# Attention of a graph and transformer kernel: the column-tiled matmuls of two steps put into one run behind the second, with a fourth buffer of weights

## What is computed

```python
q, k, v = (to_heads(q), to_heads(k), to_heads(v))
...
scores = jnp.einsum('bhqd,bhkd->bhqk', q, k) / jnp.sqrt(jnp.float32(HD))
causal = jnp.tril(jnp.ones((s, s), dtype=bool))
scores = jnp.where(causal, scores, -jnp.inf)
attn = jax.nn.softmax(scores, axis=-1)
y = jnp.einsum('bhqk,bhkd->bhqd', attn, v)
```

## Time and profile before

| | us |
|---|---|
| runs shown: median (lowest, highest) | 2546.53 (2538.53, 2550.58) |
| the profiled execution, its own time | 2537.73 |
| its span, first to last instruction | 2535.6 |
| TensorE busy, share of the span | 2115.2, 83% |
| VectorE busy | 1512.0, 60% |
| ScalarE busy | 1079.2, 43% |
| GpSimd busy | 533.2, 21% |
| mean granted clock of TensorE | 0.911 of full |

### The profile page before, as it was taken

The page is one execution under the profiler, slowest core; times in us unless marked ns, Lnnn a source line. Parts: engine busy times, 40 slices in busy tenths (PEclk is TensorE's granted clock), DMA queues, the critical chain, the costliest instruction groups (busy, mean ns, idle before and its releaser), DMA issues. The chain is left out here.

```text
span 2535.6 us, 42650 instructions
## 1 busy us (share of the span) xinstructions
PE 2115.2 (83%) x18144; PEld 1240.5 (49%) x18144; DVE 1512.0 (60%) x2332; ACT 1079.2 (43%) x1062; POOL 533.2 (21%) x442
## 2 busy tenths in 40 slices
PE   6799999999976799499999999974840599999990
PEld 3444444444432443244444444431440588888880
DVE  7778888888848169666666666601443343443423
ACT  5678888888832311023444444550210222322210
POOL 0000000000010024324555555562304000000005
PEclk9899999999988899679999999996855699999995
DMA  6311111211133213450040310007102533333307
GB/s 250 133 41 70 52 54 70 70 44 62 53 138 141 83 75 125 122 111 18 18 101 18 84 35 18 10 12 163 58 0 104 182 129 109 112 108 113 112 25 269
DMA packets 85341, 221.56 MB, mean 87 GB/s; under 512 B 9760, under 2 KB 10912, under 8 KB 78336
## 3 DMA queue, kind: packets, MB, share of 16 engines
q1 hardware_dynamic: 74064, 176.76, 21.8%
q0 software_dynamic: 11088, 42.08, 4.6%
HBM read 154.98 MB, written 59.51 MB: 85 GB/s over the span
## 5 line engine op out<-in xcount | busy, mean ns | idle before, releaser
L449 ACT ACTIVATE m_step<-m_ub,gat_bias 128x2048 bf16<-128x2048 f32 x256 | 493.9, 1992 | 119.3 <-DVE m_mask L526 105.4
L1087 DVE TENSOR_REDUCE t_rm<-t_m 128x1 f32<-128x512 f32 (+3 forms) x640 | 375.7, 609 | 203.4 <-PE t_m L1136 127.7
L1047 ACT ACTIVATE t_E<-t_s 128x1024 f32<-128x1024 f32 (+3 forms) x320 | 277.7, 894 | 368.6 <-PE t_s L1156 185.9
L526 DVE TENSOR_TENSOR m_mask<-m_step,gat_adjT 128x2048 bf16<-128x2048 bf16 x256 | 306.9, 1223 | 83.6 <-ACT m_step L449 73.4
L1026 POOL TENSOR_TENSOR t_total<-t_E 128x1024 f32<-128x1024 f32 (+2 forms) x160 | 307.8, 1936 | 167.2 <-PE t_d L1180 167.2
L1136 PE MATMUL t_m<-t_K,t_Q 96*128 96x512 f32 (+3 forms) x640 | 275.4, 452 | 55.7 <-DMA t_K<-scratch_parts 33.6
L1136 PEld LDWEIGHTS t_m<-t_K,t_Q 96*128 96x128 f32 x640 | 125.6, 200 | 208.2 <-DVE t_rm L1087 126.9
L566 PE MATMUL m_bd<-m_mask,m_S 128*32 128x512 bf16 x3072 | 211.3, 379 | 8.1 <-DVE m_mask L526 7.8
L566 PE MATMUL m_bd<-gat_adjT,m_S 128*32 128x512 bf16 x3072 | 211.3, 379 | 4.8 <-PE m_dn L566 4.8
L566 PE MATMUL m_bd<-m_mask,m_neg 128*32 128x512 bf16 x3072 | 211.1, 379 | 0.0
L1153 PE MATMUL t_s<-t_Q,t_K 97*128 97x512 f32 (+3 forms) x640 | 208.8, 402 | 0.5 <-ACT t_E L1047 0.5
(11 more groups left out here) (277 smaller groups left out, 3245.0 us busy)
## 6 DMA issues: line engine op xcount, KB each, us to landing
a_adj<-in_adj SPq DMA_DIRECT2D x16, 1024.0 KB, 5.0
m_ub<-scratch_uac SPq DMA_DIRECT2D x16, 1024.0 KB, 4.7
e_w1r<-in_L_ffn_w SPq DMA_DIRECT2D x8, 2048.0 KB, 8.2
e_w2r<-in_L_ffn_w SPq DMA_DIRECT2D x8, 2048.0 KB, 8.9
t_Q<-scratch_parts SPq DMA_DIRECT2D x48, 256.0 KB, 4.9
scratch_xe<-o_zeros POOLq DMA_DIRECT2D x10, 1024.0 KB, 19.9
e_xe<-scratch_xe SPq DMA_DIRECT2D x8, 1280.0 KB, 8.9
scratch_ye<-e_ye POOLq DMA_DIRECT2D x40, 256.0 KB, 2.3
```

The costliest lines, as they stand in the source:

```text
L449: act.activation(step[n % RELUS][:, :], ub[h % 2][:, :], ACT.Relu, bias=bias[:, j, h:h + 1], scale=BIG).then_inc(step_ready, 1)
L526: dve.tensor_tensor(mask[n % MASKS][:, :], step[n % RELUS][:, :], adjT[:, j, :], ALU.min).then_inc(mask_ready, 1)
L1047: act.activation(E[n % 3][:, two, off:BANK], ps_s[:, two, off:BANK], ACT.Exp, scale=SCALE).then_inc(exp_done[z], 1)
L1087: dve.tensor_reduce(rm[:, h, t, ch:ch + 1], ps_m[i % 2][:, 0:w], AX, ALU.max).then_inc(entry_read, 1)
```

## The change

In the attention only, and in four parts.

1. `values(n)` is no longer issued in every step. In odd steps TensorE issues `denominators(n // 2 - 1)`, `values(n - 1)` and `values(n)` in one run; in even steps none. So the array goes from whole to groups 80 times and not 160 times.
2. `t_E` has four buffers and not three, and the waits of ScalarE on values and sums are for step n-4 and not n-3.
3. `t_out` and `t_den` have one buffer each and not two, so a copy waits for the stores of the chunk just before it.
4. The partial maxima `t_rm` are kept for four row tiles and not for all sixteen.

```diff
-        E = [st.sb(f"E{i}", [P, G, BANK]) for i in range(3)]
+        E = [st.sb(f"E{i}", [P, G, BANK]) for i in range(4)]
...
-        rm = st.sb("rm", [P, G, T, NC])
+        rm = st.sb("rm", [P, G, 4, NC])
...
-        out = [st.sb(f"out{i}", [P, BANK]) for i in range(2)]
-        den = [st.sb(f"den{i}", [P, BANK]) for i in range(2)]
+        out = st.sb("out", [P, BANK])
+        den = st.sb("den", [P, BANK])
...
-                if u >= 2:
-                    act.wait_ge(d_sent[u % 2], 64 * (u // 2))
-                act.activation(den[u % 2][:, :], ps_d[:, :], ACT.Copy).then_inc(d_copied, 1)
+                if u >= 1:
+                    act.wait_ge(d_sent, 64 * u)
+                act.activation(den[:, :], ps_d[:, :], ACT.Copy).then_inc(d_copied, 1)
...
-                        if n >= 3:
-                            act.wait_ge(pv_done, n - 2)
-                            act.wait_ge(summed[z], SUMS[(n - 3) // 2 + 1])
+                        if n >= 4:
+                            act.wait_ge(pv_done, n - 3)
+                            act.wait_ge(summed[z], SUMS[(n - 4) // 2 + 1])
...
-                    if u >= 2:
-                        dve.wait_ge(o_sent[u % 2], 64 * (u // 2))
-                    dve.tensor_copy(out[u % 2][:, :], ps_o[:, :]).then_inc(o_copied, 1)
+                    if u >= 1:
+                        dve.wait_ge(o_sent, 64 * u)
+                    dve.tensor_copy(out[:, :], ps_o[:, :]).then_inc(o_copied, 1)
...
-                        if n >= 2 and n % 2 == 0:
-                            denominators(n // 2 - 1)
-                        values(n)
+                        if n % 2:
+                            if n >= 3:
+                                denominators(n // 2 - 1)
+                            values(n - 1)
+                            values(n)
```

More of the change, by code:

```diff
@@ L922, in stage_attention @@
             sem("t_" + n) for n in ("pv", "dend", "o_copied", "d_copied", "ef", "er", "m_ready", "mTr", "setup", "link"))
-        o_sent = [sem(f"t_o_sent{i}") for i in range(2)]
-        d_sent = [sem(f"t_d_sent{i}") for i in range(2)]
+        o_sent = sem("t_o_sent")
+        d_sent = sem("t_d_sent")
         with nc.Block() as block:
@@ L962, in store @@
                         row = (q * G + h) * OUT
-                        sp.dma_start(o_dram[row:row + DH, cut], out[u % 2][h * DH:(h + 1) * DH, :]).then_inc(o_sent[u % 2], 16)
+                        sp.dma_start(o_dram[row:row + DH, cut], out[h * DH:(h + 1) * DH, :]).then_inc(o_sent, 16)
                     sp.wait_ge(d_copied, u + 1)
@@ L966, in store @@
                         row = (q * G + h) * OUT + DH
-                        sp.dma_start(o_dram[row:row + 1, cut], den[u % 2][h * DH:h * DH + 1, :]).then_inc(d_sent[u % 2], 16)
+                        sp.dma_start(o_dram[row:row + 1, cut], den[h * DH:h * DH + 1, :]).then_inc(d_sent, 16)
                 for c in range(2):
@@ L997, in _ @@
                     store(q, 3)
-                for i in range(2):
-                    sp.wait_ge(o_sent[i], 64 * QUADS * NC // 2)
-                    sp.wait_ge(d_sent[i], 64 * QUADS * NC // 2)
+                sp.wait_ge(o_sent, 64 * QUADS * NC)
+                sp.wait_ge(d_sent, 64 * QUADS * NC)
             @block.gpsimd
@@ L1024, in _ @@
                         if wide < off:
-                            pool.tensor_copy(total[:, two, wide:off], E[a % 3][:, two, wide:off]).then_inc(summed[z], 1)
-                        pool.tensor_tensor(total[:, two, off:BANK], E[a % 3][:, two, off:BANK],
-                                           E[(a + 1) % 3][:, two, off:BANK], ALU.add).then_inc(summed[z], 1)
+                            pool.tensor_copy(total[:, two, wide:off], E[a % 4][:, two, wide:off]).then_inc(summed[z], 1)
+                        pool.tensor_tensor(total[:, two, off:BANK], E[a % 4][:, two, off:BANK],
+                                           E[(a + 1) % 4][:, two, off:BANK], ALU.add).then_inc(summed[z], 1)
             def denominators_out(act, u):
@@ L1042, in _ @@
                         act.wait_ge(s_full[z], n + 1)
-                        if n >= 3:
-                            act.wait_ge(pv_done, n - 2)
-                            act.wait_ge(summed[z], SUMS[(n - 3) // 2 + 1])
+                        if n >= 4:
+                            act.wait_ge(pv_done, n - 3)
+                            act.wait_ge(summed[z], SUMS[(n - 4) // 2 + 1])
                         two = slice(2 * z, 2 * z + 2)
-                        act.activation(E[n % 3][:, two, off:BANK], ps_s[:, two, off:BANK], ACT.Exp,
+                        act.activation(E[n % 4][:, two, off:BANK], ps_s[:, two, off:BANK], ACT.Exp,
                                        scale=SCALE).then_inc(exp_done[z], 1)
@@ L1086, in entry @@
                     h, t, ch, w = what
[L1087 removed]
+                    dve.tensor_reduce(rm[:, h, t % 4, ch:ch + 1], ps_m[i % 2][:, 0:w], AX, ALU.max).then_inc(entry_read, 1)
                     c = t // 4
@@ L1167, in values @@
                         mm = pe.matmul(ps_o[h * DH:(h + 1) * DH, off:BANK], V[:, kt, (q * G + h) * DH:(q * G + h + 1) * DH],
-                                       E[n % 3][:, h, off:BANK], start=(kt == 0), stop=(kt == 4 * c + 3))
+                                       E[n % 4][:, h, off:BANK], start=(kt == 0), stop=(kt == 4 * c + 3))
                     mm.then_inc(pv_done, 1)
```

3 lines of the change are left out of this document (1 added, 2 removed).

## The result

| | before | changed |
|---|---|---|
| median of the runs, us | 2548.56 | 2591.02 |
| lowest to highest | 2538.53 to 2550.60 | 2588.86 to 2594.54 |
| ratio, 95% interval | | 1.0176 (1.0146 to 1.0206) |
| the profiled execution's span | 2535.6 | 2588.3 |
| mean granted clock of TensorE | 0.911 | 0.898 |

The change costs 42 us in the medians and 52.7 us between the two profiled executions. I had forecast 15. The sign was right, the size was not, and 2591 lies outside my range.

What follows compares the result with a forecast made beforehand. TensorE's order was taken as the bound, with VectorE's reads delaying entries. Terms 8.0 + 3.6 + 1.5 + 1.7 = +14.8, say +15 us, gave a forecast median of 2561 us, range 2538 to 2576.

Steps and rivals of the forecast that it cites:

- What bounds the kernel: Attention body: TensorE has a matmul under way in 507.8 of 530 us, so its order sets the time.
- The drain's 0.41 us: Each run's mode changes cost TensorE 0.41 us; removing 80 runs would save 33 us if nothing else moved.
- The rule for the join: Where two steps meet, the fifth entry waits for the third's read, 1.18 us after its start; steps 16 and 17: +0.2.
- the walk: Start-by-start count of a quad's twenty step pairs: -0.4 to +0.6 us each, together +2.8; +8.0 over the quads counted.
- The clock: Throughout the attention, the sum counted on TensorE's full granted clock, 2.4 GHz.
- the chain: Chain of the maxima at the join, steps 32 and 33: within the walk, +1.8 us at most for three pairs.
- The first quad, +3.6: Steps 2 to 19, paced by reads: nine pairs at +0.4 us each, +3.6 us, bounds -3.7 and +5.
- The single outgoing tile, +1.7: At quad ends the copy waits 1.3 us for stores behind K, twice at most: +1.7 us, bounds 0 and +5.
- The smaller `t_rm`, the fourth buffer: nothing: Neither costs: the order of reads is unchanged, and the fourth weights buffer gives ScalarE back the step of later `denominators`.
- The tail, +1.5: Steps without entries: five pairs at 6.16 us, 0.14 longer, and four masked or narrow runs: +1.5 us, bounds 0 and +5.
- The rivals: Drain alone counts, 2517 us, chance 0.15; drain and join cancel within 0.5%, chance 0.34; much slower, 2580, chance 0.08.
- much slower: Single outgoing tile makes VectorE or ScalarE wait at thirteen other chunk ends: 19 us more, 2580 us, chance 0.08.

Runs made afterwards that it cites:

- experiment 3: The kernel before, with VectorE reading only 128 columns of each entry, leaving out most of each row maximum: 2484.4 us.
- experiment 4: The changed kernel, with VectorE reading only 128 columns of each entry: 2516.5 us.
- experiment 1: The changed kernel with its runs back where they were before, the buffer changes kept: 2547.7 us, ratio 1.003 to the kernel before.
- experiment 6: The changed kernel with the maxima's sign turned in the copy out of PSUM, not by its own VectorE instruction: 2580.1 us, ratio 1.015.
- experiment 2: The changed kernel with even steps' entries placed earlier, so two and not three meet at the join: 2575.1 us, ratio 1.0133.
- experiment 5: The changed kernel with the stores of a quad's last chunk issued before the 3 MB of K: 2581.4 us, ratio 1.0151.
- experiment 7: The changed kernel with stores before K, the sign turned in the copy, and the first quad's runs not merged: 2548.6 us, ratio 1.0040.
- experiment 8: The kernel before, runs untouched, with entries also put between the two heads of a half's scores: 2526.9 us, ratio 0.9944.
- experiment 11: The kernel before with six waits added, VectorE reading one entry four times at each of six places: 2563.3 us, ratio 1.0064.

## Why the prediction was wrong

- **What bounds the kernel**: right. TensorE's order, with VectorE's reads behind it.
- **The drain's 0.41 us**: 0.33 measured, where nothing else differs. Too high by a fifth.
- **The rule for the join**: right. Steps 16 and 6 came within 0.02 us of the walk. Nineteen of a quad's twenty pairs, each taken in a quad where the clock stayed full, add up to +2.4 us, where twenty were walked at +2.8; the twentieth, steps 32 and 33, had no such quad. The rule was right about full reads; experiments 3 and 4 show that most of the join is the hand-over's latency, so shorter reads would not have saved it.
- **The clock**: the step that failed. Every term of the sum takes TensorE's work at full speed and a wait at its own length. From the second pair to the last the trace has 96.0 us at half clock in the changed kernel and 13.6 before. At half a us lost for each, that is an estimate of 41 of the 56 us by which these pairs got longer. The 15 that are left are what I had forecast for the whole, partly by luck: the same estimate leaves 1 us of the first quad (+3.6 forecast), 0.6 of the tail (+1.5), and 3.7 and 4.0 at the copy and the chain (+1.7 and 1.8 at most).
- **The first quad, +3.6**: where it failed most. Measured +19.8. I took each wait at its length. The joins add to the waits at entries there (TensorE idle 10.0 us in the nine pairs, 5.5 before), and the clock fell again and again. The windows on one such stretch of the changed kernel:

```profile
1130.00:1138.50 8.50, 7.69 (x33) 3.67 (x26) 5.49 (x9) 2.31 (x3) 3.71 (x2) 0.90 0.01 3
1138.50:1145.00 6.50, 6.50 (x30) 2.54 (x32) 2.92 (x5) 1.78 (x2) 1.10 (x1) 0.54 0.00 0
1145.00:1151.00 6.00, 5.27 (x32) 2.47 (x20) 4.26 (x8) 1.62 (x2) 3.58 (x2) 1.00 0.00 0
```

- **The single outgoing tile, +1.7**: the mechanism and both places were right. The waits are 1.9 and 2.2 us, over the 1.3 each that I gave as the most; the term is 10.5 us in the profile and about 7.5 in the medians of experiment 1. It was mis-sized mostly through the clock, again.
- **"The smaller `t_rm`, the fourth buffer: nothing"**: right, by experiment 1, where all the excess is in the two pairs of the copy. But beside them I left out that GpSimd's additions, moved by a step, now fall on VectorE's chain of the maxima (experiment 6). I had asked what a later `denominators` does to ScalarE and not to VectorE. Steps 32 and 33 cost 9.1 us for at most 1.8 walked.
- **The tail, +1.5**: +2.5. The pairs came at 6.14 as walked (6.16). The last one lost 1.9, and 1.25 in experiment 2, where the clock stayed full there; the rest was not looked at.
- **The rivals.** The one that came nearest in time (2580) was "much slower", with the single tile at thirteen further chunk ends as its mechanism. That it came near is luck: the trace has two copies waiting for a DMA and none elsewhere, and the two give a fifth of the loss. None of my rivals had the clock in it. I had read its row (1.00 in the body) and taken it as a property of the stage, where it was one of the old order, whose waits there stay under 1.4 us.

What stays open: which waits under 1.4 us tip the clock. Experiments 5, 6 and 7 have drops at steps 4, 20, 24 and 32 in changing quads with the same order of work, so it is not settled by the order alone, and no run here says by what. The kernel before has such drops too (steps 20 and 21 of its first quad, 11.10 us for 9.3 to 9.5 in experiments 1, 7, 8 and 11), and they may be part of its spread of 12 us between runs; that isn't shown.

## What to carry to other kernels

A run that switches the array's mode costs 0.33 us here, but it also is the time in which the engine behind TensorE catches up. Before merging runs, ask what reads were hidden in each, and count from an entry's start to the reuse of its bank (0.44 + the read + 0.05 us), not only the read. And price what lengthens a wait of TensorE to the size seen here (1.4 to 3 us) at twice its length or more. The order of single instructions between the waits is worth more than the switch: alternating entries with heads brought 0.6%, with no other change.

## What was not expected of the hardware

- The granted clock falls within a busy stage after one wait of TensorE, and stays at half for some us: 2.20 us waited cost 3.8 (experiment 11). It fell behind all 28 waits of 1.43 us or more, and behind 21 of 53 between 0.95 and 1.38 us, where the same wait brings it in one execution and not in the next.
- An instruction of 16 columns on VectorE took 0.94 us and not 0.17 while GpSimd added two tiles in SBUF, and ended 0.04 behind it (experiment 6).
- With reads of 0.29 us an entry's bank still comes free only 0.8 us behind its start, so a third entry in a row waits (experiments 3 and 4).
